# High parts of the first projections stored from ACT's DMA queue instead of SyncE's

## The reference

```python
x = _layernorm(tgt, n1_g, n1_b)
tgt = tgt + _block_sparse_self_attn(x, qkv_w, sa_out_w, sa_out_b, r_w1, r_b1, r_w2, r_b2)
x = _layernorm(tgt, n2_g, n2_b)
tgt = tgt + _mha_cross(x, memory, ca_in_w, ca_in_b, ca_out_w, ca_out_b)
x = _layernorm(tgt, n3_g, n3_b)
ff = jax.nn.relu(x @ ff_w1.T + ff_b1) @ ff_w2.T + ff_b2
return tgt + ff
```

## Time and profile before

| | us |
|---|---|
| median of 3 runs | 3284.16 |
| the runs | 3283.76, 3284.16, 3287.94 |
| the profiled execution: its time | 3283.73 |
| its span in the profile | 3282.0 |
| PE busy | 3014.0 (92% of the span) |
| DVE, ACT, POOL busy | 1771.1, 1226.1, 1925.3 |

### The profile page before, as it was taken

The page is one execution under the profiler, slowest core; times in us unless marked ns, Lnnn a source line. Parts: engine busy times, 40 slices in busy tenths (PEclk is TensorE's granted clock), DMA queues, the critical chain, the costliest instruction groups (busy, mean ns, idle before and its releaser), DMA issues. The chain is left out here.

```text
span 3282.0 us, 39692 instructions
## 1 busy us (share of the span) xinstructions
PE 3014.0 (92%) x15242; PEld 1982.2 (60%) x15242; DVE 1771.1 (54%) x2884; ACT 1226.1 (37%) x2307; POOL 1925.3 (59%) x999
## 2 busy tenths in 40 slices
PE   8998798999999959959999999999968999999999
PEld 6877677544444427744444444444426888888887
DVE  5354455677777727738777777777623222122220
ACT  2222121455555532213666666666642111111111
POOL 3223222588887776633888888888877533333422
PEclk9899999999999979976999999999988999999999
DMA  6454753544555225553242424243023010110100
GB/s 231 148 172 156 196 181 128 111 108 106 120 119 119 59 83 185 199 148 77 67 89 56 100 52 101 55 90 67 11 79 117 26 39 13 39 39 26 39 13 13
DMA packets 199538, 310.17 MB, mean 95 GB/s; under 512 B 15011, under 2 KB 93363, under 8 KB 199347
## 3 DMA queue, kind: packets, MB, share of 16 engines
q1 hardware_dynamic: 199350, 307.64, 34.4%
HBM read 189.04 MB, written 117.44 MB: 93 GB/s over the span
## 5 line engine op out<-in xcount | busy, mean ns | idle before, releaser
L1255 POOL TENSOR_TENSOR e_probs<-e_probs 128x2048 f32<-128x2048 f32 x160 | 731.4, 4579 | 189.7 <-ACT e_probs L1231 184.9
L1231 ACT ACTIVATE e_probs<-e_st 128x512 f32<-128x512 f32 x1024 | 557.4, 598 | 408.5 <-PE e_st L1413 390.6
L1309 DVE TENSOR_REDUCE e_neg_max<-e_nat 128x1 f32<-128x1024 f32 x512 | 602.2, 1218 | 169.8 <-PE e_nat L1396 164.9
L1231 ACT ACTIVATE b_probs<-b_st 128x512 f32<-128x512 f32 (+3 forms) x768 | 340.3, 491 | 280.6 <-PE b_st L1413 271.7
L1306 DVE CUSTOM_DVE_ANT_0 b_nat<-b_nat,mask_qk 128x128 f32<-128x128 f32 (+7 forms) x512 | 374.4, 784 | 82.5 <-PE b_nat L1396 81.3
L1413 PE MATMUL e_st<-e_qs,e_ks 98*128 98x512 f32 x1024 | 395.5, 430 | 10.5 <-DMA e_qs<-e_max_lo 7.2
L1255 POOL TENSOR_TENSOR b_probs<-b_probs 128x1536 f32<-128x1536 f32 (+3 forms) x128 | 374.8, 2928 | 38.5 <-PE b_pv L1425 35.6
L1716 POOL TENSOR_TENSOR m_hid_lo<-m_hid,m_hid_hi 128x512 fp32r<-128x512 f32 x128 | 168.3, 1315 | 390.3 <-DVE m_hid_hi L1753 390.3
L1396 PE MATMUL e_nat<-e_ks,e_qs 96*128 96x512 f32 x1024 | 345.9, 422 | 40.2 <-DMA e_vs<-cv 25.4
L1753 DVE CAST m_hid_hi<-m_hid 128x512 fp32r<-128x512 f32 x128 | 58.8, 459 | 570.0 <-ACT m_hid L1632 570.0
L1413 PEld LDWEIGHTS e_st<-e_qs,e_ks 98*128 98x128 f32 x1024 | 175.8, 189 | 263.7 <-ACT e_probs L1231 195.9
(11 more groups left out here) (180 smaller groups left out, 5197.9 us busy)
## 6 DMA issues: line engine op xcount, KB each, us to landing
b_qs<-sq_hi SPq DMA_DIRECT2D x32, 512.0 KB, 6.9
b_ks<-sk_hi SPq DMA_DIRECT2D x32, 512.0 KB, 14.8
e_qs<-cq_hi SPq DMA_DIRECT2D x32, 512.0 KB, 6.8
e_ks<-ck_hi SPq DMA_DIRECT2D x32, 512.0 KB, 14.6
ck_hi<-p_part_hi SPq DMA_DIRECT2D x32, 256.0 KB, 2.6
ck_lo<-p_part_lo SPq DMA_DIRECT2D x32, 256.0 KB, 2.6
cv<-p_tok_out SPq DMA_DIRECT2D x32, 256.0 KB, 3.0
p_x<-in_x SPq DMA_DIRECT2D x8, 1024.0 KB, 7.5
```

Source lines behind the costliest of these rows:

```text
L1231: act.activation(probs[:, home(n, k), j, first:TOK], st_ps[:, bank_at("scores", blk), first:TOK], ACT.Exp).then_inc(exped, 1)
L1255: pool.tensor_tensor(into, into, probs[:, home(n, k), :, first:TOK], ALU.add).then_inc(added, 1)
L1309: dve.tensor_reduce(neg_max[:, u:u + 1], found, AX.XY, ALU.max, negate=True).then_inc(maxed, 1)
```

## The change

The high part's store moves from SP's program to ACT's, right behind the rounding that makes it. ACT waits for its own rounding to have finished, through `hi_ready`, and then issues the DMA. SP keeps the low parts, the values and all loads, and no longer waits for `hi_ready`. Buffers, semaphores, destinations and the count of DMAs stay the same.

```diff
@@ -341,9 +341,7 @@
             b, s = i % self.CTX // HALVES, i % HALVES
             if kind == "chan":
                 n = self.first_chan(i) + k
-                _, _, hi, lo = self.chans[i >= self.CTX][k]
-                sp.wait_ge(self.hi_ready, n + 1)
-                sp.dma_start(hi[b, s], self.part_hi[:, n % self.PARTS, :].bitcast(F32)).then_inc(self.part_stored[n % self.PARTS], 16)
+                lo = self.chans[i >= self.CTX][k][3]
                 sp.wait_ge(self.lo_ready, n + 1)
                 sp.dma_start(lo[b, s], self.part_lo[:, n % self.PARTS, :].bitcast(F32)).then_inc(self.part_stored[n % self.PARTS], 16)
             elif k == SUB - 1:
@@ -403,6 +401,10 @@
                 n = self.first_chan(i) + k
                 act.wait_ge(self.emptied, self.first_item(i) + q + 1)
                 act.copy(self.part_hi[:, n % self.PARTS, :], self.full[:, n % self.PARTS, :]).then_inc(self.hi_ready, 1)
+
+                act.wait_ge(self.hi_ready, n + 1)
+                act.dma_start(self.chans[i >= self.CTX][k][2][i % self.CTX // HALVES, i % HALVES],
+                              self.part_hi[:, n % self.PARTS, :].bitcast(F32)).then_inc(self.part_stored[n % self.PARTS], 16)
```

## The result

| | before | changed |
|---|---|---|
| median, us | 3284.16 | 3294.95 |
| lowest to highest of 11 runs each | 3281.21 to 3288.77 | 3286.22 to 3303.86 |
| profiled execution: time, span | 3283.73, 3282.0 | 3286.22, 3284.5 |
| its mean granted clock | 0.959 | 0.962 |

The ratio is 1.0033, with a 95% interval of 1.0022 to 1.0043: the changed kernel is 10.8 us slower, 7 to 14 by the interval.

What follows compares the result with a forecast made beforehand. PE was taken as the bound in the memory tiles. Bursts +7.4 and tile 11's loads +3.4, together 10.8 on a median of 3284.16, gave 3295.0 us; range 3284 to 3302, 8 in 10.

Steps and rivals of the forecast that it cites:

- The bursts, +7.4: Memory tiles 0, 1, 2 and 5: ACT's issues between four late roundings delay the copy PE needs; +7.4 us together.
- The clock, counted as none: Tiles 1, 2 and 5: clock may fall to half after new idle; none in the sum, 3.4 us for the range.
- The loads, +3.4: Tile 11: five more high parts served beside the 14 loads, ahead of the low part PE awaits; +3.4 us.
- stores may slip in: Tile 11, from the other side: stores go where loads leave engines unused; low part lands at 408.1, gain of 1.4.
- Nothing in x tiles: X tiles: PE waits for DVE before chunk 0 anyway, longer than ACT's 0.48 us; no effect counted.
- nothing for SP's 96 issues fewer: SP issues 96 DMAs fewer, each 0.32 us, on nobody's path except behind tile 11's loads; nothing counted elsewhere.
- (a): ACT's issue is nearly free: bursts 1.8, loads 0 to 3.4; 3286 to 3289.4 us, no measurable change; chance 0.25.
- (b): Everything at its upper bound: bursts 9.4, loads 6.3, two falls of the clock 3.4; 3303 us; chance 0.10.
- (c): Tile 11: low part comes free, PE's 12.26 us idle and half clock go, -15.1; 3276.5 us, faster; chance 0.07.
- (d): Queues not separated: ACT's DMAs served in one row with SP's, bursts alone count; 3291.6 us, slower; chance 0.08.

## Why the prediction was right, and where it was not

The forecast was 3295.0 and the median 3294.95, slower by 10.8 us as forecast. That the number met so closely is luck in its parts: one term was a little too small, the second should have been nothing, and the clock, which was counted as none, by my estimate stood in for it.

*The bursts, +7.4.* The mechanism is shown: the cost sits in the memory tiles (10.4 of 10.8), it vanishes when the issues move behind the copies, vanishes when no burst forms, and grows when the issues double. The step by step price was nearly right: 1.02 an item against 1.00, the issue 0.33 against 0.32, the lost overlap 0.13 against 0.12. A burst lengthened by 2.0 instead of 1.9, which makes 7.8 instead of 7.4. PE's waits grew by 9.3, of which 1.4 is tile 0's, where the clock of that execution had brought PE there earlier; against the fairer base they grew by 8.1.

*The clock, counted as none.* The prediction named falls behind tiles 1, 2 and 5 and kept two of them for its range. Two came in the changed kernel's profile, behind tiles 2 and 5, worth some 3.2 us. In the profiles of the memory tiles alone and of the low parts by ACT there is one, behind tile 2; in those of the kernel before, the x tiles alone, the deferred stores and the wait alone there is none at either place. As an estimate that is 1.6 to 3.2 us on top of 8.1, which makes 9.7 to 11.3 and takes in the measured 10.8. The interval of 7 to 14 can't confirm it more closely, and other falls come and go from one execution to the next.

*The loads, +3.4.* This is the term that failed. The step was "stores are added and the engines have no free share". The share of 1.06 is time in which an engine has a packet under way; it did not mean that nothing more could be moved. Beside the loads at 208 GB/s the high parts went through too, 252 GB/s in all at the same share, and DVE's wait stayed at 19.61 and PE's at 12.3 instead of growing to 15.7. My lower bound, "stores may slip in", was the nearer one; its -1.4 did not come either.

*Nothing in x tiles, nothing for SP's 96 issues fewer.* Right: the x tiles alone gave a ratio of 0.9998, and with both costs hidden the two kernels take 3262.15 and 3262.38.

*Rivals.* (a), a nearly free issue, falls by the 0.33 in the rows; but the deferred stores show that it is free where no wait drains ACT first. (b) did not come. (c), a gain in tile 11, did not come: the change left the low part behind the loads, and the high parts' leaving did not bring it forward. Its price was nearly right. It put the wait and the half clock behind it at 15.1, and the run in which ACT issues the low parts themselves gave 15.5 to 15.9. (d) falls with the same run, and the changed kernel's page has the second queue.

An issue on ACT takes 0.33 us in the rows here. The Trainium skill (DMA: Bandwidth & Descriptors, the table under the anatomy of one DMA) gives about 50 ns for the sequencer's dispatch, but for DMAs that GpSimd issues, so it does not price this one. Its rule that a DMA engine takes turns between queues (the same page, Queues, rings and completion order) agrees with the low part on ACT's queue landing at 390.2, ahead of a load that was issued before it. The sentence that the prediction took from the same page of the Trainium skill (Issuing engines are not separate DMA queues), that issuing from more engines saves only the sequencer's issue time, holds here with a large number in it: SP's issuing was held 11.54 us for two loads. Beyond it, the two queues together moved 252 GB/s where SP's alone moved 208.

## What to carry to other kernels

Before a DMA issue is put on a compute engine, look for the places where that engine is late and works off a burst, and at what stands behind the burst; average load (22% here) says nothing of it. If the issue must wait for the engine's own last result, put it a few instructions later: here the same stores then cost nothing. Where an engine near its bound waits longer, look at its clock behind the wait too. A second queue pays only for the transfer that is really waited for, here the low part behind a block of loads; moving its twin freed nothing.

## What I had not expected

ACT goes ahead to its DMA issues while its own earlier instructions still run: with the stores behind the copies, issues began 1.4 us before an instruction that precedes them in the program, and roundings kept their 0.52. That an engine runs its own instructions in order holds here for the order in which they are handed on, not for what still runs when the next one starts. It is the wait for the rounding just handed on that turns 0.33 us of issue into 0.50 of delay. And DMA engines that are shown full at 208 GB/s took 44 GB/s of stores from the other queue without the low part behind the loads landing later.
